# Offset stage: the pixel-major rows of h1 are turned by a DMA transpose of two-byte halves instead of by TensorE

## What is computed

```python
x1 = x + proj(attention(group_norm(x)))                 # layer 0
h1 = relu(batchnorm(conv2d(x1, w1), g1, b1))            # layer 1, 3x3
off = conv2d(h1, w_off) + b_off                         # 18 offsets per pixel
out = relu(batchnorm(deform_conv(h1, off, w2), g2, b2) + x1)
```

## Time and profile before

| | us |
|---|---|
| median of 3 executions | 2383.05 (2382.85 to 2387.11) |
| profiled execution, own time | 2383.99 |
| its span in the trace | 2382.2 |
| offset stage, from ScalarE's first L682 to the first window load | 1698.5 to 1810.2 |
| PE busy, share of the span | 95% |
| DVE, ACT, POOL busy | 76%, 76%, 61% |

### The profile page before, as it was taken

One profiled execution on the slowest core, in us unless ns is written; L12 is line 12 of the kernel. 1 busy time (PEld: TensorE's weight loads), 2 busy tenths in 40 slices (PEclk: granted clock), 3 DMA queues, 4 the chain that ended last, 5 costly groups with the idle time before them and its releaser, 6 DMA issues.

```text
span 2382.2 us, 73210 instructions
## 1 busy us (share of the span) xinstructions
PE 2259.9 (95%) x26668; PEld 1823.1 (77%) x26668; DVE 1807.8 (76%) x3885; ACT 1801.3 (76%) x2968; POOL 1449.4 (61%) x1103
## 2 busy tenths in 40 slices
PE   5999999999999999999999999979898999999992
PEld 2677777777777777777777777768667999999992
DVE  6778877777877777877777777668676887878885
ACT  5788888888888888888888888733376777777774
POOL 3669656666655666665666666685125665666660
PEclk9999999999999999999999999989899999999996
DMA  2878888878988788988877777785135443443437
GB/s 90 191 171 168 177 181 162 175 176 172 180 185 153 175 177 173 177 164 150 172 177 175 177 176 174 174 265 163 29 81 146 121 126 113 125 121 120 123 99 282
DMA packets 1048758, 377.62 MB, mean 159 GB/s; under 512 B 975489, under 2 KB 1035522, under 8 KB 1040386
## 3 DMA queue, kind: packets, MB, share of 16 engines
q1 hardware_dynamic: 1048578, 375.35, 67.7%
HBM read 98.69 MB, written 41.68 MB: 59 GB/s over the span
## 4 chain that ended last, share of the span: by engine, by line
PE 74%; POOL 10%; issue 7%; DVE 3%; DMA 3%; ACT 1%; SPq 0%; POOLq 0%; DVEq 0%; ACTq 0%
PE psum L1116 14%; PE psum L1117 14%; PE psum L1118 14%; POOL probs_split L399 10%; PE psum L1156 7%; PE psum L1158 7%; PE psum L1157 7%; PE psum L1293 5%; PE psum L1272 2%; DMA probsT_dma<-probs_split 2%; PE psum L1142 2%; PE psum L1280 1%; DMA final<-x_scratch 1%; DVE neg_max L776 1%; PE psum L1262 0%
## 5 line engine op out<-in xcount | busy, mean ns | idle before, releaser
L399 POOL TENSOR_TENSOR probs_split<-probs,probs_split 128x896 f16<-128x896 f32 x512 | 966.6, 1888 | 525.2 <-ACT probs_split L571 525.2
L776 DVE TENSOR_REDUCE neg_max<-psum 128x1 f32<-128x1024 f32 x512 | 626.2, 1223 | 308.4 <-PE psum L1118 306.1
L568 ACT ACTIVATE probs<-psum,exp_bias 128x1024 f32<-128x1024 f32 x512 | 570.5, 1114 | 184.2 <-DVE exp_bias L778 183.2
L1156 PE MATMUL psum<-vT_hi,probsT_dma 128*128 128x129 f16 x3584 | 637.6, 221 | 9.5 <-DMA probsT_dma<-probs_split 9.5
L1158 PE MATMUL psum<-vT_hi,probsT_dma 128*128 128x129 f16 x3584 | 637.3, 219 | 0.0
L1157 PE MATMUL psum<-vT_lo,probsT_dma 128*128 128x128 f16 x3584 | 637.2, 218 | 0.0
L571 ACT ACTIVATE probs_split<-probs 128x896 f16<-128x896 f32 x512 | 486.5, 950 | 22.9 <-ACT probs L568 1.0
L507 POOL TENSOR_TENSOR interp<-row_hats,col_hats 128x360 f32<-128x360 f32 x384 | 295.2, 797 | 184.8 <-PE psum L1293 173.9
L1116 PE MATMUL psum<-k_hi,q_hi 128*128 128x512 f16 x1024 | 388.9, 380 | 4.3 <-DVE q_lo L892 2.5
L1117 PE MATMUL psum<-k_lo,q_hi 128*128 128x512 f16 x1024 | 389.1, 380 | 0.0
L1118 PE MATMUL psum<-k_hi,q_lo 128*128 128x512 f16 x1024 | 389.1, 380 | 0.0
(11 more groups left out here) (177 smaller groups left out, 4911.8 us busy)
## 6 DMA issues: line engine op xcount, KB each, us to landing
xt_windows<-xt_scratch SPq DMA_DIRECT2D x192, 320.0 KB
xt_scratch<-zeros_f SPq DMA_DIRECT2D x28, 576.0 KB, 4.3
probsT_dma<-probs_split SPq DMA_TRANSPOSE x512, 3.5
x_residual<-x SPq DMA_DIRECT2D x128, 64.0 KB, 2.4
x_scratch<-x_out SPq DMA_DIRECT2D x128, 64.0 KB, 2.1
x_rows<-x_scratch SPq DMA_DIRECT2D x32, 256.0 KB, 3.4
xt_scratch<-xt_stage SPq DMA_DIRECT2D x128, 64.0 KB
final<-x_scratch SPq DMA_DIRECT2D x16, 512.0 KB, 10.0
```

The lines of the kernel that those rows point to most:

```text
L399: po.tensor_tensor(PH[j][:, 1, :], P[:, j, 0:128 * DT[j]], PH[j][:, 0, :], ALU.subtract).then_inc(s["pl"], 1)
L568: act.activation(P[:, j, :], sc, ACT.Exp, bias=NB[:, par, j:j + 1]).then_inc(s["exp"], 1)
L776: ve.tensor_reduce(NM[:, par, j:j + 1], sc, AX.X, ALU.max, negate=True).then_inc(s["mx"], 1)
L1156: pe.matmul(dst, th, Vh[:, p, v, 0:129], start=n == 0, stop=False)
```

## The change

`HT` is split into halves while it still lies channel-major. A new buffer `XI` ("xt_halves", two buffers by parity) takes, for each r, 128 high halves and 128 low halves: ScalarE's `h1_staged` writes the high ones, VectorE the low ones. SyncE then turns all eight tiles of 128 x 128 halves with one DMA transpose per block, from `XI` into `XS`, and issues the four stores when that has landed. TensorE's four transposes, their waits and the semaphore `xt` are gone; there is a new pair of semaphores `s_xi` (a transpose has landed).

SyncE's list is now: wait for `xe` of block m and for the stores of block m-2 (they free `XS`), issue the transpose of block m, wait for the transpose of block m-1, issue the four stores of block m-1. ScalarE's `h1_staged` of block m waits for the transpose of block m-2 (it frees `XI`) where it waited for the stores of m-2. ScalarE may overwrite an `HT` buffer when VectorE has read it (`xe`), where before TensorE's `xt` was enough.

```diff
+        XI = sb_in(l1, "xt_halves", [128, 2, TW, 2, 128], F16)
...
+        s_xi = [sem(f"xt_dma_transposed{i}") for i in range(2)]
...
-            for b in range(B):
-                for rb in range(NCH):
-                    after(sp, "xe", b * NCH + (rb + 1))
-                    for r in range(TW):
-                        slot = (b * IMG_ROWS + (GUARD + 8 * rb)) * PITCH + (1 + r * SLOTS)
-                        dst = bass.AP(xt_dram.tensor, slot * (2 * C), [[PITCH * 2 * C, 8], [2 * C, WW // TW], [1, 2 * C]])
-                        sp.dma_start(dst, XS[:, rb % 2, r, :]).then_inc(s_xs[rb % 2], 16)
+            def xt_store(m):
+
+                b, rb = divmod(m, NCH)
+                stored(sp, s_xi[rb % 2], m // 2 + 1)
+                for r in range(TW):
+                    slot = (b * IMG_ROWS + (GUARD + 8 * rb)) * PITCH + (1 + r * SLOTS)
+                    dst = bass.AP(xt_dram.tensor, slot * (2 * C), [[PITCH * 2 * C, 8], [2 * C, WW // TW], [1, 2 * C]])
+                    sp.dma_start(dst, XS[:, rb % 2, r, :]).then_inc(s_xs[rb % 2], 16)
+
+            for m in range(B * NCH):
+                after(sp, "xe", m + 1)
+                stored(sp, s_xs[m % 2], (m // 2) * TW)
+                sp.dma_start_transpose(XS[:, m % 2, :, :].rearrange("p r (e c) -> p (r e) c", e=2),
+                                       XI[:, m % 2, :, :, :].rearrange("p r e i -> p (r e i)")).then_inc(s_xi[m % 2], 16)
+                if m:
+                    xt_store(m - 1)
+            xt_store(B * NCH - 1)
...
-            for k in s_xo + s_xs + s_tr:
+            for k in s_xo + s_xs + s_tr + s_xi:
...
-            after(po, "xt", B * NCH)
+            after(po, "xe", B * NCH)
...
-            def h1_staged(m, par):
-                after(act, "xt", m + 1)
-                act.wait_ge(s_xs[par], (m - par) * 32 + OPEN)
-                src = PS[:, 4 + par, :].rearrange("p (t c) -> p t c", c=C)
-                act.activation(XS[:, par, :, 0:C], src, ACT.Copy).then_inc(s["xth"], 1)
+            def h1_staged(m, par, at):
+                after(act, "hA", m + 1)
+                act.wait_ge(s_xi[par], (m - par) * 8 + OPEN)
+                src = HT[:, at, :].rearrange("p (i r) -> p r i", r=TW)
+                act.activation(XI[:, par, :, 0, :], src, ACT.Copy).then_inc(s["xth"], 1)
...
-                        after(act, "xt", n - 3)
+                        after(act, "xe", n - 3)
...
-                        src = PS[:, 4 + rb % 2, :].rearrange("p (t c) -> p t c", c=C)
-                        xs = XS[:, rb % 2, :, :]
-                        ve.tensor_tensor(xs[:, :, C:2 * C], src, xs[:, :, 0:C], ALU.subtract).then_inc(s["xe"], 1)
+                        src = HT[:, (rb + 2) % 4, :].rearrange("p (i r) -> p r i", r=TW)
+                        xi = XI[:, rb % 2, :, :, :]
+                        ve.tensor_tensor(xi[:, :, 1, :], src, xi[:, :, 0, :], ALU.subtract).then_inc(s["xe"], 1)
...
-                        after(pe, "hA", n + 1)
-                        after(pe, "xe", n - 1)
-                        for r in range(TW):
-                            src = HT[:, rb % 4, :].rearrange("p (i r) -> p r i", r=TW)[:, r, :]
-                            last = pe.transpose(PS[:, 4 + rb % 2, 128 * r:128 * r + 128], src, ident)
-                        last.then_inc(s["xt"], 1)
```

More of the change, by code:

```diff
@@ L227, in build @@
             hA="h1_ready", hp="h1_split", of="offset_conv", oe="offset_rows_ready", ot="offset_transposed",
-            ocp="offset_copied", xt="h1_transposed", xth="h1T_hi_ready", xe="h1T_ready",
+            ocp="offset_copied", xth="h1T_hi_ready", xe="h1T_ready",
             hd="distances", hb="distances_abs", hx="hats_ready", pr="interp_ready", fin="offset_steps", sh="pass_shift",
@@ L683, in offset_image @@
                     if rb < NCH + 2 and (rb >= 2 or not first):
-                        h1_staged(n - 2, rb % 2)
+                        h1_staged(n - 2, rb % 2, (rb + 2) % 4)
                     if rb < NCH + 3 and (rb >= 3 or not first):
```

## The result

The changed kernel takes 2460.57 us (2459.15 to 2461.39, four executions) against 2383.72 us for the kernel before (2382.85 to 2387.11) beside it: a ratio of 1.032, with a 95% interval of 1.0307 to 1.0332. That is 77 us slower. The prediction was 2440, with a range of 2420 to 2472.

What follows compares the result with a forecast made beforehand. TensorE set the offset stage's pace at 3.19 us a block; after the change SP's list would, at 5.2 us. That delays the window loads by 60 us, less 3 at the head: net +57, 2440 us, range 2420 to 2472.

Steps and rivals of the forecast that it cites:

- Step 1: In SP's list per block, issuing the DMA transpose of 8 tiles: 0.85 us, between bounds of 0.60 and 1.48.
- Step 2: In SP's list, the wait for the transpose of block m-1: costs nothing, except at the very end.
- Steps 3 and 4: In SP's list, four stores, 1.92 us from first start to last; then the wait for their landing, 2.36 us.
- The round: SP's list for one block of the offset stage: 5.2 us against 3.19 before, bounds 4.5 to 6.3.
- The end of the stage: From the issue of block 31's transpose at 1862 to the first window load at 1870: 7.9 us.
- The head of the pass: From first window load to first matmul on a window: only loads left, 5.7 us, so 3 us taken back (0 to 5).
- ScalarE and VectorE: The two splits reading HT in SBUF with a stride: no change from 594 and 683 ns; upper bounds also cost nothing.
- TensorE's clock: In the offset stage it may fall to the low level: 5.0 us a block, still under 5.2, so no cost.
- the faster side: Rival in the offset stage: SP keeps up, TensorE's 20 us are gained, the kernel takes 2363 us; chance 0.03.
- The landing is hidden: Rival: SP is bound by issues alone, 3.4 us a block, 2386 us, no change; chance 0.03.
- The transpose tile by tile: Rival: the DMA transpose works through tiles one after another, 10.5 us a block, 2600 us; chance 0.02.
- The dearer transpose: Rival: stores queue behind the transpose's bytes or its issue costs more; round 6.3 to 8 us, 2473 to 2524; chance 0.10.

Runs made afterwards that it cites:

- xs4: The changed kernel with four buffers of XS in place of two, and four semaphores for the stores: 2412.29 us, ratio 1.011 to the kernel before.
- the last kernel: The changed kernel with four XS buffers, two of four stores issued by GpSimd, and halves copied into XI from PDh and PDl: 2389.90 us, ratio 1.0029.

## Why the prediction came out as it did

The mechanism was right in each part that carries the sum: TensorE's 20 us gained nothing, SP's list became the bound, and the wait for its own stores, one step old, was the largest piece. The time came out 20 us above the point, inside the range. Of these 20 us the rounds make 15 and the head of the pass 3; some 2 are not placed.

- **Step 1, the issue of the transpose: mis-sized.** I took 0.85 us, in proportion to the tiles; it is 1.23 us, and the cut in two showed that it hardly depends on them. Thirty rounds of 0.38 us are 11 of the 20 us. The upper bound of 1.48, the nearest row, was the better guide than a slope drawn through one point.
- **Step 2** was right: the stores of a block follow the issue of the next transpose within 0.05 us, so the wait for the one before costs nothing.
- **Steps 3 and 4** were right: 1.92 us for the starts, 2.3 us to landing (2.27 in the chain above, 2.36 taken). SP's own wait is shorter than the 2.3 us that I named as the sign, 1.66 us, because the landing is counted from the start of the last store's issue, and that holds SP for 0.60. The experiments with the wait alone put in (+32 us) and taken out (-48 us) show it from both sides. The two differ because the rounds do: from TensorE's pace up in the one, 3.27 to 4.37 us, and down to SP's issues in the other, 5.66 to 3.9.
- **The round** was to be 5.2 us and is 5.53 where nothing disturbs it. The mean from the transpose of block 2 (1710.98) to that of block 31 (1875.19) is 5.66, since in some rounds an issue took longer, such as 2.23 us for a transpose at 1733.96. No row says why. The mean round's 0.46 us too much, 29 times, is 13 us; the first rounds add 2.
- **The end of the stage:** from the last transpose's issue to the first window load I had 7.9 us; it is 1883.06 - 1875.19 = 7.87. Part of that agreement is luck: the issue took 0.4 us more than I had, and the way from the last store's start (1880.96) to the first load 2.1 us in place of 2.5.
- **The head of the pass: wrong.** I took back 3 us, since only the loads would be left to wait for. They take 1891.20 - 1883.06 = 8.1 us, as good as the 8.4 of the earlier trace rows. The step that failed is the 5.7 us for three loads: I had divided 162 GB/s by the share of 0.58, as if the engines would be full, and from 1883.0 to 1891.2 us they moved 158 GB/s at a share of 0.56. The chain has a load of 6.85 us to landing, the last in front of the first matmul.
- **ScalarE and VectorE:** the splits take 1.11 and 1.07 us, inside the bounds of 0.6 to 1.2 and 0.7 to 1.4, though I had taken no change. It cost nothing here, as forecast, because both engines wait for SP. Beyond the change it is part of what holds back a repaired version.
- **TensorE's clock** fell to 0.70 in the mean of 1704 to 1760 us, and with work put back on TensorE the time stayed: no cost, as said.

Of the rivals, the faster side (issues that cost SP next to nothing) is refuted by xs4, in which SP does nothing but issue, without a gap, for 3.91 us a block. *The landing is hidden* did not hold for the change, and its price was too low too: with the landing hidden, in xs4, the round is 3.91 us and not 3.4, and the kernel is 27 us slower than before, not level with it. The transpose tile by tile is refuted by a landing in 3.1 us for eight tiles. That the Trainium skill's figure, quoted with that rival, is the price of a lone tile is not shown; no run has a transpose of one. The dearer transpose, at a round of 6.3 us and more, has a grain of truth in step 1, but its mechanism, stores delayed by the transpose's bytes, is not seen: they land in 2.3 us as before.

## What to carry to other kernels

Before moving work from a full engine to DMA, write down the issuing queue's list for one round: every issue with its duration, and every wait on something that the same queue issued a step before. Such a wait puts a whole landing in the round; let it be for something older, with more buffers (here four in place of two took it out). Then compare the issues alone with the engine's round: 3.84 us against 3.19 was too much even so. The issue of a DMA transpose was priced nearly by the instruction and not by the tile, so few and large ones are the cheaper way to use it.

## What the runs showed of the hardware

- Issue of a DMA transpose on SP: 1.27, 1.23 and 1.48 us for 4, 8 and 14 tiles of 128 x 128 f16; landing in 2.5, 3.1 and 3.5 us. With the DMA engines busy for 0.87 of the time, eight tiles land in 3.8 us.
- A plain store of 64 KB in 128 rows of 512 bytes holds GpSimd for 0.594 us, and SP for 0.603. With both issuing, in the last kernel, single stores held SP for up to 1.23 us.
- An elementwise instruction of 512 elements a partition reads f32 from SBUF with a stride of 16 bytes in 1.11 us (ScalarE) and 1.07 us (VectorE), where the same from PSUM, contiguous, took 0.594 and 0.683, and contiguous from SBUF 0.613 and 0.698. Reading f16 with a stride of 8 bytes takes ScalarE 0.697 us. Writing f16 with a stride of 512 bytes takes 2.49 us. The Trainium skill ("SBUF — State Buffer", section "Door 1: The DMA port swizzle (why `[64,N]` ≈ `[32,N]`)") gives SBUF lines of 16 bytes, of which each access to a new one pays a penalty. The f32 read agrees with the penalty: at 16 bytes every element is on a line of its own. But the same passage counts a stride of up to four f32 as free, and there the trace does not agree, with 1.07 us against 0.698. At 8 bytes two f16 share a line, and the copy is faster, but no row here has the same read without a stride to compare it with. The strided write costs more than twice that read, and the page has no figure for it.
